# Windowed attention layers on one core: the norm's floor as a maximum over pairs, its first guess on ScalarE, and a new order of four VectorE pieces

## The chip, the cores and the metric

The kernel runs on one core of a Trainium2 chip. The metric is the device time of one execution in microseconds; lower is better. Given are three runs of the kernel before and one profiled execution.

## What is computed

The input x has 4 sequences of 512 tokens with 128 channels. Six parts follow each other on it: a feed-forward part with sign weights, a rotary attention, the same feed-forward part, a stack of six windowed layers, a delta-rule memory, and the same stack of six windowed layers again. The change touches the two stacks alone. One layer of the stack:

```python
def attn_layer(x, Wqkv, qs, ksc, Wo):          # 16 heads of 64, window 32
    q, k, v = split(x @ Wqkv)
    q = l2norm(q) * qs
    k = l2norm(k) * ksc                        # l2norm(t) = t / max(|t|, 1e-12)
    q = q * cos * scale + rotate_half(q) * sin * scale
    k = k * cos * inv + rotate_half(k) * sin * inv
    return local_attention(q, k, v) @ Wo       # softmax(8 * q k^T) v over 64 keys

def ffn_layer(x, g, bln, W1, b1, W2, b2):
    xn = (x - mean(x)) / sqrt(var(x) + 1e-5) * g + bln
    a, gate = split(xn @ W1 + b1)
    return a * gelu(gate) @ W2 + b2

for i in range(6):
    x = attn_layer(shift_tokens(x), ...) + x
    x = ffn_layer(shift_tokens(x), ...) + x
```

## The kernel before

`windowed_layers` runs one stack. It walks over tiles of 128 tokens: a layer has 16 of them (4 sequences of 4 tiles), a stack 96, and there are two stacks, `run` 0 and 1. Each turn of the walk is a step k, and in a step each engine works on several tiles of different ages: T is new, A one step old, B two, C three, D four. `walk` writes steps 0 to 11 out, then two turns of a loop over 32 steps, then the rest. The order of each engine's work in a step is written out by hand in its `step` function; engines meet at semaphores only.

For a tile, TensorE projects the queries of 16 heads (`project`, L251) into PSUM; ScalarE squares them (`square`, L477) into `squares`; VectorE rotates them (`rotate`: L574 with the cosines, L579 with the sines) into `turned`, which frees PSUM for the keys; then the same for the keys. VectorE sums the squares of a head (`sum_squares`, L583) into `sumsq`, 16 numbers for the queries, 16 for the keys; four more columns hold the variances of a feed-forward layer norm (L643). So 36 inverse square roots are wanted per step. VectorE raises `sumsq` to at least 1e-24 (L654, the floor), makes the first guess by integer arithmetic on the bits (L656) and -0.5 times the sum (`halved`, L657). GpSimd does three Newton steps of four instructions (`invert_roots`, L713 to L723), in the next step of the walk. GpSimd also adds the two parts of the rotation (`add`, L703) and multiplies by the inverse norms (`normalise`, L732).

Attention for older tiles: TensorE transposes queries and keys of B (`turn`, L257), ScalarE copies them out (L511, L518); `scores` (L269, L277) gives the scores of B, VectorE takes the negated maximum (L661) and adds it (L667) into `probs`. One step later, for what is then C, ScalarE takes exp (L506), VectorE the row sums (L602) and their inverse (L606), GpSimd multiplies (L740, `pool_p`), VectorE transposes (`pT`, L623), TensorE multiplies by the tokens (`gather`, L287), ScalarE copies to `px` (L481) and TensorE applies the merged weights (`output`, L295).

The feed-forward part of a sequence is spread over steps by k mod 4. At k mod 4 = 3 VectorE adds the attention's result to Z (L679) and TensorE does the up products of an earlier sequence (L415, with `hidden`, L595, on VectorE between them). At 0 TensorE does the down product (L317), VectorE adds it to Z (L616), and TensorE centres the next sequence (L356) and takes its variance (L374). At 1 it broadcasts the inverse deviation (L403), after which VectorE forms `xn` (L588). At 2 come the gate products (L410).

TensorE's order in a step: project the queries of T; transpose the queries of B; `place_0` (the down product, or tokens transposed, L264, which at k mod 4 = 2 wait for `xn`); five pairs of `output`; transpose the keys of B; more `output`; `place_1` (centring, first gate or up product); project the keys of T, which waits for the first rotation; `gather`; `place_2`; the last `output`; `scores`; `place_3`.

VectorE's order in a step: row sums and inverse of C; rotation of the queries of T; at 0 the additions into Z; transposition of C; square sums of the queries; hidden rows; rotation of the keys; square sums of the keys; floor, guess and halves; maximum and difference of B; `xn`, the last hidden rows, or the additions of the attention's result.

Of the kernel before, what the change touches and what calls it, by code (L numbers as in the profile page):

```python
# [6 lines left out]
P = 128  # L7
# [3 lines left out]
I32 = mybir.dt.int32  # L11
ALU = mybir.AluOpType
ACT = mybir.ActivationFunctionType
AXX = mybir.AxisListType.X
# [3 lines left out]
TILES = SEQ // P  # L18
PER = BATCH * TILES
EPS = 1e-5  # L20

DEPTH, HEADS, DH, WIN = 6, 16, 64, 32
# [7 lines left out]
FFB = -(-FF // P)  # L30
VEC = 3 + 2 * FFB
MASKED = -3.0e38
ROOT_BITS, NEWTONS = 0x5F3759DF, 3


EDGE = 96
# [102 lines left out]
def windowed_layers(nc, run, sem, Z, consts, dram):  # L139
# [6 lines left out]
    with ctx:  # L146
        def sb(name, shape, dt=F32):
            return ctx.enter_context(nc.sbuf_tensor(f"{tag}_{name}", shape, dt))
# [14 lines left out]
        rot_l = sb("rot_l", [P, 2, 2, 2, TILES, DH])  # L163
        squares = sb("squares", [P, 2, INNER])
        turned = sb("turned", [P, 2, 2, INNER])
        sumsq = sb("sumsq", [P, NORMS])
        bits = sb("bits", [P, NORMS], I32)
        newton = sb("newton", [P, NORMS])
        halved = sb("halved", [P, NORMS])
        c_1_5, c_zero, c_seed = sb("c_1_5", [P, NORMS]), sb("c_zero", [P, NORMS]), sb("c_seed", [P, NORMS])  # L170
        inv_norm = sb("inv_norm", [P, NORMS])
        rstd = sb("rstd", [P, TILES])
        qk = sb("qk", [P, 2, 2, INNER])
# [6 lines left out]
        row_inv = sb("row_inv", [P, HEADS])  # L180
        pT = sb("pT", [P, 2, HEADS, WIN])
        px = sb("px", [P, 2, WINS, HEADS, WIN])
        warm = sb("warm", [P, 1])
        xn = sb("xn", [P, SEQ])
        xn_sq = sb("xn_sq", [P, SEQ])
        hid = sb("hid", [P, FFB, SEQ])
# [6 lines left out]
        pe_cen, pe_var, pe_bc, pe_gate = sem("pe_cen"), sem("pe_var"), sem("pe_bc"), sem("pe_gate")  # L193
        pe_up, pe_down, pe_bias = sem("pe_up"), sem("pe_down"), sem("pe_bias")
        act_sq, act_tq, act_tk, act_xt = sem("act_sq"), sem("act_tq"), sem("act_tk"), sem("act_xt")
        act_px, act_exp, act_m = sem("act_px"), sem("act_exp"), sem("act_m")
        act_cen, act_gate, act_gelu = sem("act_cen"), sem("act_gate"), sem("act_gelu")
        dve_turn, dve_ss, dve_floor, dve_guess = [sem(s) for s in ("dve_turn", "dve_ss", "dve_floor", "dve_guess")]
        dve_max, dve_sub, dve_sum, dve_inv, dve_pt = sem("dve_max"), sem("dve_sub"), sem("dve_sum"), sem("dve_inv"), sem("dve_pt")
        dve_y, dve_var, dve_xn, dve_hid, dve_z, dve_bias = [  # L200
            sem(s) for s in ("dve_y", "dve_var", "dve_xn", "dve_hid", "dve_z", "dve_bias")]
# [270 lines left out]
        def _(act):  # L472
# [27 lines left out]
            def step(s):  # L500
                T, B, C, D = s.T, s.B, s.C, s.D
                if T:
                    square(T, 0, pe_q)
                if C:
                    act.wait_ge(dve_sub, C.n + 1)
                    nc.scalar.activation(probs[:], probs[:], ACT.Exp).then_inc(act_exp, 1)  # L506
                if B:
                    act.wait_ge(pe_tq, B.n + 1)
                    if C:
                        act.wait_ge(pe_s, C.n + 1)  # L510
                    nc.scalar.activation(flat(qT[:]), flat(ps_t[:]), ACT.Copy).then_inc(act_tq, 1)  # L511
                    if s.k % TILES:
                        tokens_out(B)
                    act.wait_ge(pe_tk, B.n + 1)
                    if s.k == B_LAG:
                        act.wait_ge(cleared, run + 1)
                    turned_k = ps_t[:, :, :].rearrange("p a (b q) -> p (a b) q", q=P)
                    nc.scalar.activation(kT[:, :, HALO + B.t * P:HALO + (B.t + 1) * P], turned_k,  # L518
                                         ACT.Copy).then_inc(act_tk, 1)
                if s.up:  # L520
                    f = s.up
                    act.wait_ge(act_gate, f.m * FFB + FFB)
                    nc.scalar.activation(flat(hid[:]), flat(hid[:]), ACT.Gelu).then_inc(act_gelu, 1)
                if s.merge():
                    layer, parity, quarters = s.merge()
                    merged(layer, parity, quarters[0])
                if s.cen:
                    f = s.cen
                    act.wait_ge(pe_cen, f.m + 1)
                    nc.scalar.activation(xn_sq[:], ps_f[:], ACT.Square)  # L530
                    nc.scalar.activation(xn[:], ps_f[:], ACT.Copy).then_inc(act_cen, 1)
                if s.gate:
                    gate(s.gate, 0)
                if T:
                    square(T, 1, pe_k)
                if C:
                    act.wait_ge(pe_px, C.n + 1)
                    if D and D.k:
                        act.wait_ge(pe_y, D.n)
                    gathered(C, 0)  # L540
                if s.merge():
                    merged(layer, parity, quarters[1])
                if s.gate:
                    gate(s.gate, 1)
                if C:
                    gathered(C, 1)
                if s.up:
                    nc.scalar.activation(warm[:], c_1_5[:, 0:1], ACT.Exp)
                if s.gate:
                    gate(s.gate, 2)  # L550
                if B and s.k % TILES == 0:
                    tokens_out(B)

            walk(act, run, step)

        @block.vector
        def _(dve):
# [3 lines left out]
            ends = Z[:, EDGE:EDGE + BATCH * SPAN].rearrange("p (b t) -> p b t", b=BATCH)  # L561
            nc.vector.memset(ends[lower, :, SEQ:SPAN], 0.0)
            nc.vector.memset(ends[upper, :, 0:1], 0.0)
            nc.vector.memset(c_zero[:], 0.0)
            nc.vector.memset(c_seed[:], float(ROOT_BITS))
            nc.vector.memset(sumsq[:], 1.0).then_inc(edged, 1)
            dve.wait_ge(edged, run + 1)

            def rotate(T, which):
# [10 lines left out]
                                        swapped, sin, ALU.mult).then_inc(dve_turn, 1)  # L580

            def sum_squares(T, which):
                nc.vector.reduce_sum(sumsq[:, which * HEADS:(which + 1) * HEADS], squares[:, which, :]  # L583
                                     .rearrange("p (h d) -> p h d", d=DH), AXX).then_inc(dve_ss, 1)

            def normal(f):
# [10 lines left out]

            def step(s):
                T, A, B, C, D = s.T, s.A, s.B, s.C, s.D
                if C:  # L600
                    dve.wait_ge(act_exp, C.n + 1)
                    nc.vector.reduce_sum(row_sum[:], probs[:], AXX).then_inc(dve_sum, 1)  # L602
                    dve.wait_ge(dve_sum, C.n + 1)
                    if D:
                        dve.wait_ge(pool_p, C.n)
                    nc.vector.reciprocal(row_inv[:], row_sum[:]).then_inc(dve_inv, 1)  # L606
                if T:
                    if T.k % PER == 0:
                        dve.wait_ge(pool_rot, T.layer + 1)
                    rotate(T, 0)  # L610
                if s.down:
                    f = s.down
                    dve.wait_ge(pe_down, f.m + 1)
# [5 lines left out]
                if C:  # L619
                    dve.wait_ge(pool_p, C.n + 1)  # L620
                    if D:
                        dve.wait_ge(pe_px, D.n + 1)
                    nc.vector.transpose(pT[:].rearrange("p a h q -> p h a q"),  # L623
                                        probs[:].rearrange("p h (a k) -> p h a k", a=2)).then_inc(dve_pt, 1)
                if T:
                    if s.chain_before is not None:
                        dve.wait_ge(dve_guess, s.chain_before + 1)
                    sum_squares(T, 0)
                if s.up:
                    hidden(s.up, 0)  # L630
                if s.bias():
# [8 lines left out]
                if s.cen:  # L640
                    f = s.cen
                    dve.wait_ge(pe_var, f.m + 1)
                    nc.vector.tensor_scalar(sumsq[:, 2 * HEADS:NORMS], ps_f[:, 0:TILES], EPS, None,  # L643
                                            ALU.add).then_inc(dve_var, 1)
                if T:
                    sum_squares(T, 1)
                if s.chain is not None:
                    if T:
                        dve.wait_ge(dve_ss, T.n * 2 + 2)
                    if s.cen:  # L650
                        dve.wait_ge(dve_var, s.cen.m + 1)
                    if s.k:
                        dve.wait_ge(pool_inv, s.chain)
                    nc.vector.scalar_tensor_tensor(sumsq[:], sumsq[:], 1e-24, sumsq[:], ALU.max, ALU.max).then_inc(dve_floor, 1)  # L654
                    dve.wait_ge(dve_floor, s.chain + 1)
                    nc.vector.scalar_tensor_tensor(bits[:], sumsq[:].bitcast(I32), -0.5, c_seed[:], ALU.mult, ALU.add)  # L656
                    nc.vector.scalar_tensor_tensor(halved[:], sumsq[:], -0.5, c_zero[:], ALU.mult,  # L657
                                                   ALU.add).then_inc(dve_guess, 1)
                if B:
                    dve.wait_ge(pe_s, B.n + 1)  # L660
                    nc.vector.tensor_reduce(neg_max[:], ps_heads, AXX, ALU.max, negate=True).then_inc(dve_max, 1)  # L661
# [24 lines left out]
        def _(pool):  # L686
# [17 lines left out]
                                        ALU.add).then_inc(pool_add, 1)  # L704

            def invert_roots(chain, bc):
                pool.wait_ge(dve_guess, chain + 1)
                y = bits[:].bitcast(F32)
                for k in range(NEWTONS):
                    at = chain * (4 * NEWTONS - 1) + 4 * k  # L710
# [1 line left out]
                        pool.wait_ge(pool_newton, at)  # L712
                    nc.gpsimd.tensor_tensor(newton[:], y, y, ALU.mult).then_inc(pool_newton, 1)  # L713
                    pool.wait_ge(pool_newton, at + 1)
                    nc.gpsimd.tensor_tensor(newton[:], newton[:], halved[:], ALU.mult).then_inc(pool_newton, 1)
                    pool.wait_ge(pool_newton, at + 2)
                    nc.gpsimd.tensor_tensor(newton[:], newton[:], c_1_5[:], ALU.add).then_inc(pool_newton, 1)
                    pool.wait_ge(pool_newton, at + 3)
                    if bc and k == NEWTONS - 1:
                        rows = slice(2 * HEADS, NORMS)  # L720
# [39 lines left out]
def rotary_tables():  # L760
# [8 lines left out]
    both = lambda a, b: np.concatenate([a, b], -1)  # L769
    cos, sin = np.cos(freqs), np.sin(freqs)  # L770
    rows = []
    for s in (8.0 * scale, 1.0 / scale):
        rows.append([both(cos * s, cos * s), both(-sin * s, sin * s)])
    rows = np.array(rows).astype(np.float32)
    rows = rows.reshape(2, 2, TILES, P, DH).transpose(3, 0, 1, 2, 4)
# [1424 lines left out]
```

## Time and profile before

| | |
|---|---|
| three runs | 4502.45 us median (4500.79 to 4517.26) |
| profiled execution | 4515.56 us, of which the span is 4513.4 us |
| TensorE busy | 4068.2 us (90%) |
| VectorE busy | 3318.9 us (74%) |
| GpSimd busy | 2748.9 us (61%) |
| ScalarE busy | 2057.4 us (46%) |
| mean granted TensorE clock | 0.936 of full |

The two stacks take about 1650 us each (from 560 to 2215 us and from 2775 to 4415 us of the span); there the granted clock is 0.99. Shares of busy time are means over the whole span, the stacks' waits are in the rows below. PEld is TensorE's weight load. Times are microseconds from the span's start unless said otherwise.

### The profile page before, as it was taken

How to read it: one execution, taken by the hardware profiler on the slowest of the kernel's cores; microseconds unless marked ns; L12 is line 12 of the kernel's file. 1: busy time of each engine (PE TensorE's matmuls, PEld its weight loads, DVE VectorE, ACT ScalarE, POOL GpSimd, SP SyncE). 2: the span in 40 equal slices, each digit the busy share in tenths (PEclk: the TensorE clock that was granted, in tenths of full speed). 3: DMA queues.
4: the chain of work that ended last, by engine and by line, in shares of the span. 5: the costliest groups of instructions: out<-in, count | busy, mean ns of one | idle time of the engine just before them, and what ended most of it. 6: DMA issues, size and time to landing. Idle time of an engine off the chain costs nothing. (4 is left out here: it accounts for less than half of the span.)

```text
span 4513.4 us, 129963 instructions
## 1 busy us (share of the span) xinstructions
PE 4068.2 (90%) x56144; PEld 2601.6 (58%) x56144; DVE 3318.9 (74%) x3855; ACT 2057.4 (46%) x2429; POOL 2748.9 (61%) x3481
## 2 busy tenths in 40 slices
PE   8999889999999999999867776999999999999996
PEld 4333456566666666666536663666656666666663
DVE  1575288888888888888734334888888888888883
ACT  2454245554545555555421112455555555554552
POOL 0000188777777777777614124878777777787781
PEclk9999899999999999999976556999999999999997
DMA  0000100000000000000000001000000000000000
GB/s 18 1 1 1 47 11 11 11 16 11 2 17 11 16 11 2 7 2 2 2 7 4 4 4 57 11 11 2 17 11 17 12 2 17 11 7 2 2 2 10
DMA packets 14118, 46.29 MB, mean 10 GB/s; under 512 B 3808, under 2 KB 6240, under 8 KB 11744
## 3 DMA queue, kind: packets, MB, share of 16 engines
q1 hardware_dynamic: 13536, 37.83, 2.4%
q8 instruction: 450, 7.37, 0.7%
q14 instruction: 132, 1.08, 0.1%
HBM read 36.78 MB, written 1.05 MB: 8 GB/s over the span
## 5 line engine op out<-in xcount | busy, mean ns | idle before, releaser
L703 POOL TENSOR_TENSOR w_qk<-w_turned 128x1024 f32<-128x1024 f32 x384 | 906.7, 2361 | 152.9 <-DVE w_turned L579 151.7
L251 PE MATMUL w_ps_qk<-w_w_qk,ZT 128*128 128x512 f32 x1536 | 764.0, 621 | 74.5 <-DVE w_turned L579 52.0
L295 PE MATMUL w_ps_y<-w_px,w_w_vo 128*128 128x128 f32 x6144 | 788.3, 277 | 6.1 <-DVE ZT L679 6.1
L295 PEld LDWEIGHTS w_ps_y<-w_px,w_w_vo 128*128 128x128 f32 x6144 | 744.1, 192 | 80.4 <-issue 76.6
L477 ACT ACTIVATE w_squares<-w_ps_qk 128x1024 f32<-128x1024 f32 x384 | 393.4, 1024 | 753.0 <-PE w_ps_qk L251 753.0
L732 POOL TENSOR_TENSOR w_qk<-w_qk,w_inv_norm 128x1024 f32<-128x1024 f32 x384 | 723.0, 1905 | 0.0
L574 DVE TENSOR_TENSOR w_turned<-w_ps_qk,w_rot_l 128x1024 f32<-128x1024 f32 x384 | 467.4, 1217 | 239.5 <-ACT w_squares L477 213.7
L740 POOL TENSOR_TENSOR w_probs<-w_probs,w_row_inv 128x1024 f32<-128x1024 f32 x192 | 365.5, 1904 | 347.1 <-DVE w_row_inv L606 346.5
L251 PEld LDWEIGHTS w_ps_qk<-w_w_qk,ZT 128*128 128x128 f32 x1536 | 281.9, 195 | 404.0 <-issue 312.0
L481 ACT ACTIVATE w_px<-w_ps_w 128x1024 f32<-128x1024 f32 x384 | 379.2, 1021 | 199.8 <-PE w_ps_w L287 199.8
L579 DVE TENSOR_TENSOR w_turned<-w_ps_qk,w_rot_l 128x1024 f32<-128x1024 f32 x384 | 466.1, 1214 | 0.0
L583 DVE TENSOR_REDUCE w_sumsq<-w_squares 128x16 f32<-128x1024 f32 x384 | 458.2, 1193 | 0.0
L257 PEld LDWEIGHTS w_ps_w<-ident,w_qk 128*128 128x128 f32 x3072 | 353.5, 142 | 128.8 <-issue 128.7
L257 PE MATMUL w_ps_w<-ident,w_qk 128*128 128x128 f32 x3072 | 403.1, 275 | 22.7 <-ACT w_qT L511 22.5
L287 PE MATMUL w_ps_w<-w_pT,w_x_tok 32*128 32x512 f32 x3072 | 389.7, 622 | 13.4 <-issue 8.3
L518 ACT ACTIVATE w_kT<-w_ps_w 128x1024 f32<-128x1024 f32 x192 | 196.7, 1024 | 386.8 <-PE w_ps_w L257 386.8
L602 DVE TENSOR_REDUCE w_row_sum<-w_probs 128x16 f32<-128x1024 f32 x192 | 234.3, 1220 | 188.2 <-ACT w_probs L506 187.1
L690 POOL TENSOR_TENSOR w_rot_l<-w_rot,w_qk_scale 128x256 f32<-128x256 f32 x24 | 17.5, 729 | 533.3 <-DMA w_qk_scale<-in_qk_scale 533.3
L277 PEld LDWEIGHTS w_ps_w<-w_kT,w_qT 64*32 64x32 f32 x24576 | 256.3, 105 | 126.7 <-issue 126.7
L277 PE MATMUL w_ps_w<-w_kT,w_qT 64*32 64x64 f32 x24576 | 292.2, 225 | 40.4 <-issue 40.4
L654 DVE SCALAR_TENSOR_TENSOR w_sumsq<-w_sumsq 128x36 f32<-128x36 f32 x196 | 283.4, 1446 | 6.8
L287 PEld LDWEIGHTS w_ps_w<-w_pT,w_x_tok 32*128 32x128 f32 x3072 | 140.8, 186 | 247.2 <-issue 245.6
(247 smaller groups left out, 6314.8 us busy)
## 6 DMA issues: line engine op xcount, KB each, us to landing
w_w_qk<-in_w_qk SPq DMA_DIRECT2D x12, 1024.0 KB, 4.8
w_w_vT<-in_w_vT SPq DMA_DIRECT2D x12, 512.0 KB, 4.1
w_w_o<-in_w_o SPq DMA_DIRECT2D x12, 512.0 KB, 5.1
w_w<-in_w SPq DMA_DIRECT2D x12, 384.0 KB, 3.2
w_w<-in_w SPq DMA_DIRECT2D x12, 192.0 KB, 3.2
XT<-in_x SPq DMA_DIRECT2D x1, 1024.0 KB, 4.8
w_rot<-in_rot SPq DMA_DIRECT2D x2, 512.0 KB, 5.7
out<-XT SPq DMA_DIRECT2D x1, 1024.0 KB, 3.9
```

The lines of the kernel that those rows point to most:

```text
L251: last = nc.tensor.matmul(ps_qk[:, c, :], Z[:, T.col:T.col + P], w_qk[:, T.parity, cols], start=True, stop=True)
L257: last = nc.tensor.transpose(ps_t[:, p // 4, (p % 4) * P:(p % 4 + 1) * P], qk[:, B.odd, which, p * P:(p + 1) * P], ident[:])
L277: last = nc.tensor.matmul(ps_heads[w * WIN:(w + 1) * WIN, h * PAIRS + p, :], qT[rows, p, w * WIN:(w + 1) * WIN], kT[rows, p, col:col + KEY ...
L287: last = nc.tensor.matmul(ps_w[:, w, :], x_tok[rows, C.t, half, :], pT[rows, half].rearrange("p h q -> p (h q)"), start=half == 0, stop=ha ...
L295: last = nc.tensor.matmul(ps_y[:, D.t * P:(D.t + 1) * P].rearrange("p (w q) -> p w q", q=WIN), w_vo[:, D.parity, h, p, :], px[:, D.odd, :, ...
L477: nc.scalar.activation(squares[:, which, :], flat(ps_qk[:]), ACT.Square).then_inc(act_sq, 1)
L481: nc.scalar.activation(px[:, C.odd, pair].rearrange("p w h q -> p (w h q)"), flat(ps_w[:, pair, :]), ACT.Copy).then_inc(act_px, 1)
L574: nc.vector.tensor_tensor(turned[:, which, 0, :].rearrange("p (h d) -> p h d", d=DH), flat(ps_qk[:]).rearrange("p (h d) -> p h d", d=DH), ...
L579: nc.vector.tensor_tensor(turned[:, which, 1, :].rearrange("p (h two d) -> p h two d", two=2, d=HALF), swapped, sin, ALU.mult).then_inc(dv ...
L583: nc.vector.reduce_sum(sumsq[:, which * HEADS:(which + 1) * HEADS], squares[:, which, :] .rearrange("p (h d) -> p h d", d=DH), AXX).then_i ...
L703: nc.gpsimd.tensor_tensor(qk[:, T.odd, which, :], turned[:, which, 0, :], turned[:, which, 1, :], ALU.add).then_inc(pool_add, 1)
L732: nc.gpsimd.tensor_tensor(heads, heads, spread(inv, 2, [P, HEADS, DH]), ALU.mult).then_inc(pool_qk, 1)
```

## The change

The floor and the guess: `sumsq` gets a second column beside each number, filled once with 1e-24, and the floor becomes one reduction by maximum over the pairs into a tensor `floor`. The guess moves from VectorE to ScalarE: one activation (identity, scale -0.5, a bias) on the bits of `floor`, behind ScalarE's second copy to `px`, waiting for the floor; GpSimd waits for it there. `halved` goes: the square roots are taken of half the value (the variances are halved at their making, the constant of the guess is shifted by half an exponent, the query table carries 16 in place of 8), and GpSimd's third Newton instruction becomes a subtraction from 1.5.

The order on VectorE: the rotation of the queries now stands ahead of the row sums of C, and the square sums of the queries right behind the inverse, ahead of the additions into Z and the transposition.

```diff
-ROOT_BITS, NEWTONS = 0x5F3759DF, 3
+ROOT_BITS, NEWTONS = 0x5F3759DF - 0x400000, 3
...
-        sumsq = sb("sumsq", [P, NORMS])
+        sumsq, floor, seed = sb("sumsq", [P, NORMS, 2]), sb("floor", [P, NORMS]), sb("seed", [P, 1])
...
                 if s.up:
-                    nc.scalar.activation(warm[:], c_1_5[:, 0:1], ACT.Exp)
+                    nc.scalar.activation(warm[:], warm_in[:], ACT.Exp)
+                if s.chain is not None:
+                    act.wait_ge(dve_floor, s.chain + 1)
+                    if s.k:
+                        act.wait_ge(pool_inv, s.chain)
+                    nc.scalar.activation(bits[:], floor[:].bitcast(I32), ACT.Identity, bias=seed[:, 0:1],
+                                         scale=-0.5).then_inc(act_guess, 1)
                 if s.gate:
                     gate(s.gate, 2)
...
                 T, A, B, C, D = s.T, s.A, s.B, s.C, s.D
+                if T:
+                    if T.k % PER == 0:
+                        dve.wait_ge(pool_rot, T.layer + 1)
+                    rotate(T, 0)
                 if C:
                     dve.wait_ge(act_exp, C.n + 1)
                     nc.vector.reduce_sum(row_sum[:], probs[:], AXX).then_inc(dve_sum, 1)
...
                     nc.vector.reciprocal(row_inv[:], row_sum[:]).then_inc(dve_inv, 1)
                 if T:
-                    if T.k % PER == 0:
-                        dve.wait_ge(pool_rot, T.layer + 1)
-                    rotate(T, 0)
+                    if s.chain_before is not None:
+                        dve.wait_ge(dve_floor, s.chain_before + 1)
+                    sum_squares(T, 0)
                 if s.down:
...
-                if T:
-                    if s.chain_before is not None:
-                        dve.wait_ge(dve_guess, s.chain_before + 1)
-                    sum_squares(T, 0)
                 if s.up:
                     hidden(s.up, 0)
...
-                    nc.vector.scalar_tensor_tensor(sumsq[:], sumsq[:], 1e-24, sumsq[:], ALU.max, ALU.max).then_inc(dve_floor, 1)
-                    dve.wait_ge(dve_floor, s.chain + 1)
-                    nc.vector.scalar_tensor_tensor(bits[:], sumsq[:].bitcast(I32), -0.5, c_seed[:], ALU.mult, ALU.add)
-                    nc.vector.scalar_tensor_tensor(halved[:], sumsq[:], -0.5, c_zero[:], ALU.mult,
-                                                   ALU.add).then_inc(dve_guess, 1)
+                    nc.vector.tensor_reduce(floor[:], sumsq[:], AXX, ALU.max).then_inc(dve_floor, 1)
...
-                pool.wait_ge(dve_guess, chain + 1)
+                pool.wait_ge(act_guess, chain + 1)
...
-                    nc.gpsimd.tensor_tensor(newton[:], newton[:], halved[:], ALU.mult).then_inc(pool_newton, 1)
+                    nc.gpsimd.tensor_tensor(newton[:], newton[:], floor[:], ALU.mult).then_inc(pool_newton, 1)
...
-                    nc.gpsimd.tensor_tensor(newton[:], newton[:], c_1_5[:], ALU.add).then_inc(pool_newton, 1)
+                    nc.gpsimd.tensor_tensor(newton[:], c_1_5[:], newton[:], ALU.subtract).then_inc(pool_newton, 1)
```

## Rows read from the trace of the kernel before

**Rows 1.** Waits of the whole span: engine, line, releaser: total us, times, longest us
```profile
PE w_ps_qk L251 <- DVE w_turned L579: 52.0, 50, 2.4
...
PE w_ps_f L317 <- DVE w_hid L595: 44.7, 38, 2.8
...
PE w_ps_w L277 <- issue: 40.4, 31, 2.1
...
PE w_ps_f L264 <- DVE w_xn L588: 36.6, 38, 1.7
```

**Rows 2.** Timeline of TensorE, four steps of run 1: start, us, line, [idle before]
```profile
3528.58 1.88 PE L251 MATMUL w_ps_qk<-w_w_qk,ZT 128*128 128x512 f32 x4
...
3536.46 1.98 PE L251 MATMUL w_ps_qk<-w_w_qk,ZT 128*128 128x512 f32 x4
3538.37 2.00 PE L287 MATMUL w_ps_w<-w_pT,w_x_tok 32*128 32x512 f32 x16
...
3544.13 1.99 PE L251 MATMUL w_ps_qk<-w_w_qk,ZT 128*128 128x512 f32 x4
...
3548.45 0.44 PE L264 MATMUL w_ps_f<-ident,ZT 128*128 128x128 f32 x2 [1.46 <-DVE w_xn L588]
...
3555.39 2.00 PE L287 MATMUL w_ps_w<-w_pT,w_x_tok 32*128 32x512 f32 x16
...
3561.63 1.88 PE L251 MATMUL w_ps_qk<-w_w_qk,ZT 128*128 128x512 f32 x4
...
3571.40 2.00 PE L287 MATMUL w_ps_w<-w_pT,w_x_tok 32*128 32x512 f32 x16
...
3577.63 1.88 PE L251 MATMUL w_ps_qk<-w_w_qk,ZT 128*128 128x512 f32 x4
...
3581.48 2.84 PE L317 MATMUL w_ps_f<-w_hid,w_w 128*128 128x512 f32 x6 [1.09 <-DVE w_hid L595]
...
3588.12 1.13 PE L356 MATMUL w_ps_f<-ZT,centre 128*128 128x512 f32 x2 [0.25 <-DVE ZT L616]
...
3590.89 2.00 PE L287 MATMUL w_ps_w<-w_pT,w_x_tok 32*128 32x512 f32 x16
...
3596.93 1.88 PE L251 MATMUL w_ps_qk<-w_w_qk,ZT 128*128 128x512 f32 x4
```

**Rows 3.** Timeline of VectorE in the same stretch
```profile
3543.05 1.88 DVE L654 SCALAR_TENSOR_TENSOR w_sumsq<-w_sumsq 128x36 f32<-128x36 f32 x1
...
3545.19 1.22 DVE L661 TENSOR_REDUCE w_neg_max<-w_ps_w 128x16 f32<-128x1024 f32 x1
3546.51 1.23 DVE L667 TENSOR_TENSOR w_probs<-w_ps_w,w_neg_max 128x1024 f32<-128x1024 f32 x1
...
3548.86 1.22 DVE L602 TENSOR_REDUCE w_row_sum<-w_probs 128x16 f32<-128x1024 f32 x1 [0.47 <-ACT w_probs L506]
...
3551.45 1.22 DVE L579 TENSOR_TENSOR w_turned<-w_ps_qk,w_rot_l 128x1024 f32<-128x1024 f32 x1
3552.58 1.24 DVE L623 STREAM_TRANSPOSE w_pT<-w_probs 128x1024 f32<-128x1024 f32 x1
3553.74 1.18 DVE L583 TENSOR_REDUCE w_sumsq<-w_squares 128x16 f32<-128x1024 f32 x1
...
3581.34 1.38 DVE L679 TENSOR_TENSOR ZT<-w_ps_y,ZT 64x512 f32<-64x512 f32 x2
...
3586.56 1.50 DVE L616 SCALAR_TENSOR_TENSOR ZT<-w_ps_f,w_vec,ZT 64x512 f32<-64x512 f32 x2
```

**Rows 4.** Timeline of ScalarE in the same stretch
```profile
3546.23 1.02 ACT L477 ACTIVATE w_squares<-w_ps_qk 128x1024 f32<-128x1024 f32 x1 [3.77 <-PE w_ps_qk L251]
```

**Rows 5.** Timeline of GpSimd in the same stretch
```profile
3542.51 2.37 POOL L703 TENSOR_TENSOR w_qk<-w_turned 128x1024 f32<-128x1024 f32 x1
...
3550.51 1.91 POOL L740 TENSOR_TENSOR w_probs<-w_probs,w_row_inv 128x1024 f32<-128x1024 f32 x1 [1.22 <-DVE w_row_inv L606]
```

**Rows 6.** The page's group of the folded scales: busy, mean ns, idle before
```profile
L690 POOL TENSOR_TENSOR w_rot_l<-w_rot,w_qk_scale 128x256 f32<-128x256 f32 x24 | 17.5, 729 | 533.3 <-DMA w_qk_scale<-in_qk_scale 533.3
```

More of the change, by code:

```diff
@@ L165, in windowed_layers @@
         turned = sb("turned", [P, 2, 2, INNER])
-        sumsq = sb("sumsq", [P, NORMS])
+        sumsq, floor, seed = sb("sumsq", [P, NORMS, 2]), sb("floor", [P, NORMS]), sb("seed", [P, 1])
         bits = sb("bits", [P, NORMS], I32)
         newton = sb("newton", [P, NORMS])
-        halved = sb("halved", [P, NORMS])
-        c_1_5, c_zero, c_seed = sb("c_1_5", [P, NORMS]), sb("c_zero", [P, NORMS]), sb("c_seed", [P, NORMS])
+        c_1_5 = sb("c_1_5", [P, NORMS])
         inv_norm = sb("inv_norm", [P, NORMS])
@@ L195, in windowed_layers @@
         act_sq, act_tq, act_tk, act_xt = sem("act_sq"), sem("act_tq"), sem("act_tk"), sem("act_xt")
-        act_px, act_exp, act_m = sem("act_px"), sem("act_exp"), sem("act_m")
+        act_px, act_exp, act_m, act_guess = sem("act_px"), sem("act_exp"), sem("act_m"), sem("act_guess")
         act_cen, act_gate, act_gelu = sem("act_cen"), sem("act_gate"), sem("act_gelu")
-        dve_turn, dve_ss, dve_floor, dve_guess = [sem(s) for s in ("dve_turn", "dve_ss", "dve_floor", "dve_guess")]
+        dve_turn, dve_ss, dve_floor = sem("dve_turn"), sem("dve_ss"), sem("dve_floor")
         dve_max, dve_sub, dve_sum, dve_inv, dve_pt = sem("dve_max"), sem("dve_sub"), sem("dve_sum"), sem("dve_inv"), sem("dve_pt")
@@ L552, in step @@
                     tokens_out(B)
+            act.wait_ge(edged, run + 1)
             walk(act, run, step)
@@ L563, in _ @@
             nc.vector.memset(ends[upper, :, 0:1], 0.0)
-            nc.vector.memset(c_zero[:], 0.0)
-            nc.vector.memset(c_seed[:], float(ROOT_BITS))
-            nc.vector.memset(sumsq[:], 1.0).then_inc(edged, 1)
+            nc.vector.memset(warm_in[:], 0.0)
+            nc.vector.memset(sumsq[:, :, 0], 1.0)
+            nc.vector.memset(sumsq[:, :, 1], 1e-24)
+            nc.vector.memset(seed[:], float(ROOT_BITS)).then_inc(edged, 1)
             dve.wait_ge(edged, run + 1)
@@ L582, in sum_squares @@
             def sum_squares(T, which):
-                nc.vector.reduce_sum(sumsq[:, which * HEADS:(which + 1) * HEADS], squares[:, which, :]
+                nc.vector.reduce_sum(sumsq[:, which * HEADS:(which + 1) * HEADS, 0], squares[:, which, :]
                                      .rearrange("p (h d) -> p h d", d=DH), AXX).then_inc(dve_ss, 1)
@@ L642, in step @@
                     dve.wait_ge(pe_var, f.m + 1)
-                    nc.vector.tensor_scalar(sumsq[:, 2 * HEADS:NORMS], ps_f[:, 0:TILES], EPS, None,
-                                            ALU.add).then_inc(dve_var, 1)
+                    nc.vector.tensor_scalar(sumsq[:, 2 * HEADS:NORMS, 0], ps_f[:, 0:TILES], EPS, 0.5,
+                                            ALU.add, ALU.mult).then_inc(dve_var, 1)
                 if T:
@@ L771, in rotary_tables @@
     rows = []
-    for s in (8.0 * scale, 1.0 / scale):
+    for s in (16.0 * scale, 1.0 / scale):
         rows.append([both(cos * s, cos * s), both(-sin * s, sin * s)])
```

2 lines of the change are left out of this document (1 added, 1 removed).

## The prediction

> **What bounds the kernel now.** The page and the waits first: in them TensorE's longest waits on another engine inside the windowed layers are three, on VectorE each time: 52.0 us for the rotation (L579) ahead of the projection, 44.7 us for the hidden rows ahead of the down product, 36.6 us for `xn` ahead of the transposes of the tokens. A fourth, 40.4 us, stands ahead of the scores and is put down to no one ("issue") [rows 1]. Then TensorE's timeline over four steps. I number the kinds of step by k mod 4: 1 broadcasts, 2 gates, 3 multiplies up, 0 multiplies down and centres. P is the start of a step's first projection (L251), G that of its gather (L287). Kind 1: P 3528.58, G at P+9.79, next P at P+15.55. Kind 2: G at P+11.26, next P at +17.50. Kind 3: +9.77 and +16.00. Kind 0: +13.26 and +19.30 [rows 2]. From G to the next P TensorE runs its own list without a wait: 5.76, 6.24, 6.23 and 6.04 us. So a step costs G-P plus that constant, and the question is what sets G. Before G, kind 1 waits for the rotation (second projection at P+7.88), kind 2 for `xn` (1.46 us), kind 0 for `hid` (1.09 us) and for Z (0.25 us), kind 3 for nothing to speak of [rows 2]. TensorE sets the pace with VectorE a hair behind it: VectorE is not full, but it is late at three places.
>
> Why it is late at two of them is in VectorE's rows. The floor (L654, 36 columns) took 1.88 us and ended at 3544.93, when GpSimd's addition (L703, from 3542.51, 2.37 us) ended at 3544.88. The reduction of 1024 columns (L583) took 1.18 us while the same GpSimd line ran beside it [rows 3, 5]. The maximum over the scores (L661) started at 3545.19, though the scores were done about 3544.2, when the next projection began.
>
> The Trainium skill, page "SBUF — State Buffer", section "Who interferes with whom", says that a VectorE instruction with two SBUF inputs is held while a GpSimd instruction reads SBUF, and that tensor_reduce never contends on trn2. The first half is what these rows show. By the second the new floor is free of it; if the reduction were held too, the time would be that of the third rival below.
>
> **The change part by part.**
> *Floor and guess.* Three VectorE instructions go (L654, here 1.88 us, and L656 and L657, which fit into the 0.26 us between L654's end and L661's start), and one reduction of 72 columns comes. L583 takes 1.18 us for 1024 columns; scaled, that is 0.08, and the whole of it is the other end; I take 0.2, an estimate near the small end, since two small instructions fit into those 0.26 us [rows 3]. VectorE gets about 1.9 us here, but L661 can only start when the scores are done: in kind 2 that is 1.0 us earlier than now. The guess goes to ScalarE, behind its second copy to `px`. It waits there for the floor; behind it queue the last gate copy, `tokens_out` and the next step's square. The square starts at 3546.23, the floor would be done by 3543.3 [rows 3, 4], so a guess of 0.2 to 1.0 us (the square of 1024 columns takes 1.02) holds up nobody. GpSimd can start its Newton steps as soon as L703 ends instead of 0.47 us later: no cost. GpSimd's subtraction, the doubled constants and the tables in `rot` have the same shapes: nothing.
>
> The Trainium skill, page "ScalarE: Activation LUTs", section "Table sets: the hidden batching unit", says that the cheap functions, identity among them, lie in every table set; by that the guess brings no table load. No row quoted here shows more of it; with a load the guess would be later and the sum the same as long as it ends before the next square.
>
> *Rotation ahead of the row sums.* This is the part that costs. Now: square of the first projection starts at P+2.10 (3546.23), exp of the scores behind it (L667's end at 3547.74 to the row sum at 3548.86: 1.12 us), so the row sum starts about P+4.0 where ScalarE's order sets it (P+4.73 in kind 2, where L667 was late), then 1.65 us to GpSimd's multiplication (3548.86 to 3550.51), which takes 1.91, then 0.16, then the transposition 1.24. So pT is there 4.96 us after the row sum starts: at P+8.96, where TensorE's own order reaches the gather at P+9.77 [rows 2 to 5]. That was 0.8 us of cover. New: the square ends at P+3.12 by this row, or P+3.02 when the projection is 1.88 long; the rotation is two pieces of 1.22 us, and neighbours overlap by 0.08 (L579 ends at 3552.67, L623 starts at 3552.58): 2.36 us, P+3.05 to P+5.41; the row sum starts at P+5.33 [rows 3]; pT is there at P+10.29, the gather starts at P+10.33. The rotation has become part of the chain projection, square, rotation, row sum, inverse, GpSimd's multiplication, transposition, gather. The cover is gone and 0.55 us is owed.
>
> *Sum of squares behind the inverse.* 1.18 us, in the shadow of GpSimd's 1.91 us in kinds 1, 2 and 3, where VectorE waited for that product anyway under the new order: nothing. In kind 0 it stands ahead of the two additions into Z (1.50 us), for which TensorE's centring waits.
>
> *Per step.*
> Kind 1: the wait for the rotation ends at P+5.5, well ahead of need; the gather is bound by pT at P+10.33 instead of 9.79: +0.54.
> Kind 3: 10.33 for 9.77: +0.56.
> Kind 2: L661 starts right after the scores at P+0.1, L667 at +1.4 and ends at +2.65, `xn` is done at +3.3 (0.75 us, as long as one half of L616); TensorE's wait for it falls from 1.46 to about 0.6; the rotation starts at +3.3, pT is there at +10.5. G at P+10.5 instead of 11.26: -0.76. But this is the best case of kind 2. The 36.6 us over 48 such steps are 0.76 us on the mean, not 1.46 [rows 1]; where the wait was small the gather is bound by pT as in the other kinds. I take -0.76 + 0.70 = -0.06 for the mean step.
> Kind 0: the scores end about P-0.9, since one product of 512 columns lies between (half a projection, 0.94); L661 starts at about -0.7, L667 ends at +1.85, the last hidden rows (0.75, estimated as for `xn`) at +2.5: TensorE's wait for `hid` (1.09) is gone. Then the y additions (1.38) to P+3.8, rotation to +6.15, row sum to +7.3, inverse to +7.6, sum of squares to +8.7, Z to +10.2. The centring (L356) stood at P+10.49 (3588.12 less 3577.63) and now stands at +10.22. Of 1.09 us saved ahead of it all but 0.27 are given back: -0.27 [rows 2, 3].
>
> There are 48 steps of each kind (2 runs, 6 layers, 16 steps a layer): 48 x (0.54 - 0.06 + 0.56 - 0.27) = 48 x 0.77 = +37 us. At k mod 16 = 6 GpSimd also folds the scales (L690, 0.73 us twice, and four half-sized pieces of 0.36 to 0.73: 2.9 to 4.4 us [rows 6]). It delays its Newton steps and with them the multiplication now on the chain; ten times 0.5 us, +5. Sum +42 us. Against it: the 40.4 us ahead of the scores that nobody releases [rows 1] fall between gather and scores; a TensorE that now stands up to 1.9 us before the gather may have its instructions at hand by then. That is worth 0 to -40 us; the opposite, that these pauses were hidden in part by the `xn` and `hid` waits that go, 0 to +14. I take -14, a third of the first end. Net +28 us. The profiled execution took 4515.56 us, 4513.4 of it span and 2.2 around it, which the change leaves alone; it lies 0.3% over the median of the runs shown. 28 of 4515.56 is 0.62%; on the median 4502.45 that is 4530 us. This case's own range is 4504 (all 40 us gained) to 4558 (none gained, +14 paid).
>
> **The rivals.**
> *Faster: the gather is covered after all.* If pT came by P+9.77, for instance because the row sum slips in ahead of the rotation or the chain's handoffs are shorter than I add them, only the savings count: the three waits of 52.0, 44.7 and 36.6 us, 133 us at most, about 100 with the Z wait left: some 4400 us. It decides at 0.55 us, the amount by which my chain overshoots TensorE's own order. Against it: VectorE's order is fixed in the program, and each link of the chain is a row. 0.13, with half savings (4450) inside it.
> *No difference: pauses absorbed.* The full 40 us ahead of the scores go, or kind 0 gains its whole 1.09: 4490 to 4515 us. 0.20.
> *The floor does not get free.* If the reduction over pairs is held by GpSimd as L654 was, kinds 2 and 0 keep their lateness and pay the later row sum too: about 1.0 us more in each, 96 us at worst, 60 with cover: 4585 us. Against it: L583, one SBUF input, is never stretched beside L703 [rows 3, 5]. 0.07.
> *GpSimd becomes the bound.* Its own list is Newton, 4.0 us (L703's end 3544.88 to L740's start 3550.51, less 0.47 and 1.22 of idle time; the 0.47 is the wait for L657), then 1.91 + 2.37 + 3.8 (two of L740's size) + 2.37 [rows 5]: 14.5 us of steps of 16 to 19; a late multiplication pushes the next. It decides when a step has under 14.5 us, or where the fold (17.5 with it) meets kind 3. If it cost 0.3 us in every step: 4590 us. 0.04.
> The forecast's case keeps 0.56.
>
> **How the numbers follow.** Likeliest 4530 us. The range 4468 to 4575 leaves out the fast rival's bulk and the far ends of the slow ones, 2 in 10. A measurement of this kernel can tell about 0.5% from no change, 22.5 us: 4480 to 4525. Faster: the first rival, 0.13. Within: the second, and of the forecast's case the part under 4525, about 0.33 of it: 0.20 + 0.18 = 0.38, less a little for its tail: 0.37. Slower: 0.50.
>
> **What would show it.** The floor's mean near 0.2 us and the maximum over the scores starting within 0.2 us of the scores' end. TensorE's waits for `hid` gone, for the rotation gone, for `xn` more than halved. In their place a wait of TensorE at L287 for pT (L623): about 1.9 us in plain kind 1, 0.6 in kind 3, 0.1 to 0.6 in kind 2, none in kind 0, some 30 to 45 us in all per run; a longer wait for Z at L356. Steps of 16.1, 16.7, 16.6 and 19.0 us. I am wrong if L287 waits for nothing, if kind 0 falls under 18.5 us, or if the floor's duration still follows L703.

## The result: slower by 1.1%

The changed kernel takes 4557.01 us (median of 4 runs, 4551.45 to 4564.55) against 4503.48 us for the kernel before (4 runs): ratio 1.0114, 95% interval 1.0087 to 1.0141. The forecast was 4530 us, slower; the range went to 4575. So the sign and the mechanism held, and the size was about half of what came: 53.5 us between the medians where 28 were forecast. Between the two profiled executions it is 4552.70 less 4515.56, 37 us: the profiled run before lay 12 us over its median.

The page of the changed kernel, engines and two groups:

```profile
PE 4046.1 (89%) x56144; PEld 2615.8 (57%) x56144; DVE 3026.4 (67%) x3465; ACT 2099.3 (46%) x2625; POOL 2731.5 (60%) x3481
...
L286 PE MATMUL w_ps_w<-w_pT,w_x_tok 32*128 32x512 f32 x3072 | 400.9, 636 | 155.4 <-DVE w_pT L634 146.8
...
L634 DVE STREAM_TRANSPOSE w_pT<-w_probs 128x1024 f32<-128x1024 f32 x192 | 239.1, 1245 | 157.5 <-POOL w_probs L743 156.1
```

VectorE lost 292 us of work (3318.9 to 3026.4) and the kernel got slower. The last number of these two groups says where: the gather (L286) stood idle 146.8 us for `pT`, and the transposition that makes `pT` (L634) stood idle 156.1 us for GpSimd's multiplication. In the kernel before these two waits were 5.1 and 11.6 us. TensorE's waits, the list that answers to [rows 1]:

```profile
PE w_ps_w L286 <- DVE w_pT L634: 146.8, 144, 2.5
PE w_ps_f L355 <- DVE ZT L627: 49.8, 44, 1.6
PE w_ps_w L276 <- issue: 42.0, 34, 2.8
PE w_ps_qk L250 <- DVE w_turned L586: 16.4, 10, 1.9
```

The rotation's 52.0 us became 16.4. The wait for the hidden rows fell from 44.7 to 6.1 us, the one for `xn` from 36.6 to 13.6. The wait for Z ahead of the centring (L355) rose from 16.8 to 49.8, as the prediction said it would rise. The 40.4 us ahead of the scores are 42.0. And 146.8 us stand at the gather in 144 of 192 steps: three kinds of step out of four. TensorE's timeline over the same steps of kinds 2, 3 and 0 as in [rows 2]:

```profile
3563.88 1.98 PE L250 MATMUL w_ps_qk<-w_w_qk,ZT 128*128 128x512 f32 x4
...
3567.31 0.44 PE L263 MATMUL w_ps_f<-ident,ZT 128*128 128x128 f32 x2 [0.58 <-DVE w_xn L595]
...
3574.52 2.00 PE L286 MATMUL w_ps_w<-w_pT,w_x_tok 32*128 32x512 f32 x16 [0.19 <-issue]
...
3580.75 1.88 PE L250 MATMUL w_ps_qk<-w_w_qk,ZT 128*128 128x512 f32 x4
...
3591.26 2.00 PE L286 MATMUL w_ps_w<-w_pT,w_x_tok 32*128 32x512 f32 x16 [0.94 <-DVE w_pT L634]
...
3597.49 1.88 PE L250 MATMUL w_ps_qk<-w_w_qk,ZT 128*128 128x512 f32 x4
...
3607.50 1.12 PE L355 MATMUL w_ps_f<-ZT,centre 128*128 128x512 f32 x2 [1.12 <-DVE ZT L627]
...
3610.27 2.00 PE L286 MATMUL w_ps_w<-w_pT,w_x_tok 32*128 32x512 f32 x16
...
3616.30 1.88 PE L250 MATMUL w_ps_qk<-w_w_qk,ZT 128*128 128x512 f32 x4
```

The letters are those of the prediction: P is the start of a step's first projection, G that of its gather, and the kind of a step is k mod 4. Kind 2: G at P+10.64, step 16.87. Kind 3: P+10.51, step 16.74. Kind 0: the centring at P+10.01, G at P+12.78, step 18.81. From G to the next P there are 6.23, 6.23 and 6.03 us, as before. VectorE in the step of kind 3 (P = 3580.75):

```profile
3583.90 1.23 DVE L581 TENSOR_TENSOR w_turned<-w_ps_qk,w_rot_l 128x1024 f32<-128x1024 f32 x1 [1.45 <-ACT w_squares L476]
3585.04 1.22 DVE L586 TENSOR_TENSOR w_turned<-w_ps_qk,w_rot_l 128x1024 f32<-128x1024 f32 x1
3586.17 1.21 DVE L613 TENSOR_REDUCE w_row_sum<-w_probs 128x16 f32<-128x1024 f32 x1
3587.41 0.26 DVE L617 RECIPROCAL w_row_inv<-w_row_sum 128x16 f32<-128x16 f32 x1
3587.58 1.16 DVE L590 TENSOR_REDUCE w_sumsq<-w_squares 128x16 f32<-128x1024 f32 x1
3589.75 1.25 DVE L634 STREAM_TRANSPOSE w_pT<-w_probs 128x1024 f32<-128x1024 f32 x1 [1.01 <-POOL w_probs L743]
```

Here is the whole chain: VectorE is idle 1.45 us for the square, rotates, takes the row sum only at P+5.42, and later waits 1.01 us for GpSimd. `pT` is there at 3591.00, P+10.25, and the gather starts 0.26 us after that.

The means of all steps from the fifth on (44 or 46 of a kind), in us, from the starts of the first projection and of the gather in either trace; change and forecast are those of the step:

| kind (k mod 4) | G-P before, after | step before, after | change | forecast |
|---|---|---|---|---|
| 1 | 9.78, 10.46 | 16.38, 17.33 | +0.95 | +0.54 |
| 2 | 10.61, 10.54 | 17.16, 17.15 | -0.01 | -0.06 |
| 3 | 9.98, 10.55 | 16.67, 17.20 | +0.53 | +0.56 |
| 0 | 13.03, 12.60 | 19.16, 18.79 | -0.37 | -0.27 |

### The profile page after: what moved, and what is told of

It is laid out like the page before. It is cut to its first block and busy times, and to the rows that moved or that the text cites. A ratio compares the mean times of both kernels' runs of the same rounds, so it can differ in the third digit from the quotient of the medians.

```text
span 4550.9 us, 129901 instructions
## 1 busy us (share of the span) xinstructions
PE 4046.1 (89%) x56144; PEld 2615.8 (57%) x56144; DVE 3026.4 (67%) x3465; ACT 2099.3 (46%) x2625; POOL 2731.5 (60%) x3481
## 5 line engine op out<-in xcount | busy, mean ns | idle before, releaser
L250 PE MATMUL w_ps_qk<-w_w_qk,ZT 128*128 128x512 f32 x1536 | 750.7, 612 | 37.8 <-DVE w_turned L586 16.4
L743 POOL TENSOR_TENSOR w_probs<-w_probs,w_row_inv 128x1024 f32<-128x1024 f32 x192 | 365.1, 1902 | 591.2 <-DVE w_row_inv L617 590.7
L286 PE MATMUL w_ps_w<-w_pT,w_x_tok 32*128 32x512 f32 x3072 | 400.9, 636 | 155.4 <-DVE w_pT L634 146.8
L664 DVE TENSOR_REDUCE w_neg_max<-w_ps_w 128x16 f32<-128x1024 f32 x192 | 235.1, 1225 | 291.9 <-PE w_ps_w L276 286.6
L286 PEld LDWEIGHTS w_ps_w<-w_pT,w_x_tok 32*128 32x128 f32 x3072 | 156.2, 189 | 387.6 <-issue 385.9
L634 DVE STREAM_TRANSPOSE w_pT<-w_probs 128x1024 f32<-128x1024 f32 x192 | 239.1, 1245 | 157.5 <-POOL w_probs L743 156.1
```

The costliest lines, as they stand in the source:

```text
L250: last = nc.tensor.matmul(ps_qk[:, c, :], Z[:, T.col:T.col + P], w_qk[:, T.parity, cols], start=True, stop=True)
L286: last = nc.tensor.matmul(ps_w[:, w, :], x_tok[rows, C.t, half, :], pT[rows, half].rearrange("p h q -> p (h q)"), start=half == 0, stop=ha ...
```

## The experiments

The theory: the new floor and guess gain, the new order loses more, and it loses at the gather through the chain projection, square, rotation, row sum, inverse, multiplication, transposition. Seven kernels take it apart. Ratios are to the kernel before, run again beside them: 4512.71 us (13 runs) for the first four, 4510.16 us (7 runs) for the last three.

**The floor and guess alone.** The changed kernel with VectorE's old order (this cut and those below are shortened; T, C and `s.down` stand for the tiles and sequences of the step):

```diff
 def step(s):
-    if T: rotate(T, 0)
     if C: row sums, inverse
+    if T: rotate(T, 0)
-    if T: sum_squares(T, 0)
     if s.down: additions into Z
     if C: transposition
+    if T: sum_squares(T, 0)
```

> The new floor and guess with VectorE's old order (row sums first, square sums behind the transposition). My theory (the order costs, the floor gains): steps of kind 1 stay at 15.55 us, kind 2 loses most of its 0.76 us wait for xn, kind 3 is unchanged, kind 0 loses its 1.09 us wait for the hidden rows and the centring starts about 1.3 us earlier; the gather waits for pT in almost no step. In all about -75 us: ratio to before 0.983 (0.977 to 0.990). Rival (the wait at the gather comes from the guess on ScalarE or from the new floor, not from the order): near the changed kernel, 1.008 to 1.012.

Measured: 4429.38 us, ratio 0.9818 (0.9801 to 0.9834). TensorE's waits there:

```profile
PE w_ps_qk L250 <- DVE w_turned L586: 53.5, 50, 2.4
PE w_ps_w L276 <- issue: 34.4, 26, 1.9
PE w_ps_f L355 <- DVE ZT L623: 20.2, 43, 1.6
...
PE w_ps_w L286 <- DVE w_pT L630: 14.4, 10, 2.6
...
PE w_ps_f L263 <- DVE w_xn L595: 13.5, 26, 0.5
```

The ratio is where the theory put it. The gather's wait falls from 146.8 to 14.4 us by the order of VectorE alone; the guess on ScalarE is in this kernel and makes nothing late. Kind 0 takes 18.15 us on the mean (19.16 before), kind 2 16.63 (17.16), kinds 1 and 3 are unchanged (16.34 and 16.60). So the floor and guess were worth 1.8%, and the order cost 1.0114 over 0.9818, 3.0%.

**The order alone.** The kernel before, floor, guess and halves untouched, with the new order of the four pieces (the reverse of the diff above, in the kernel before).

> The new order alone, with the kernel before's floor, guess and halves. My theory: the floor still ends when GpSimd's addition ends, which the late multiplication has itself pushed back; the maximum over the scores starts 1.4 to 2.0 us after the scores in kinds 1 and 2. In all 60 to 115 us over the changed kernel: ratio to before 1.025 to 1.037. Rival (the floor is in the shadow once the order is new, VectorE has time to spare): as the changed kernel, 1.011.

Measured: 4647.59 us, ratio 1.0295 (1.0278 to 1.0312). The two halves make up the whole: 0.9818 x 1.0295 = 1.0108, and the whole change measured 1.0114. The size was forecast right and the place wrong. The excess over the changed kernel was expected in kinds 1 and 2; it is mostly in kind 0, 20.09 us on the mean against 18.79. Kind 2 has 17.52 against 17.15, kind 3 17.33 against 17.20, kind 1 nothing. The maximum starts late behind the scores of kinds 2 and 3 (1.58 and 1.42 us on the mean, 0.65 and 0.43 behind the others), so it is the steps after these that find VectorE late. What holds the floor is seen in a step where GpSimd has two pieces queued (VectorE, then GpSimd):

```profile
3637.23 0.84 DVE L654 SCALAR_TENSOR_TENSOR w_sumsq<-w_sumsq 128x36 f32<-128x36 f32 x1
3638.10 2.28 DVE L656 SCALAR_TENSOR_TENSOR w_bits<-w_sumsq,w_c_seed 128x36 int32<-128x36 int32 x1
```

```profile
3634.26 3.76 POOL L732 TENSOR_TENSOR w_qk<-w_qk,w_inv_norm 128x1024 f32<-128x1024 f32 x2
3637.98 2.36 POOL L703 TENSOR_TENSOR w_qk<-w_turned 128x1024 f32<-128x1024 f32 x1
```

The floor ends at 3638.07, when the normalisation ends (3638.02); the guess ends at 3640.38, when the addition ends (3640.34). With two GpSimd instructions behind each other, two small VectorE instructions are held in a row.

**The squares back.** The changed kernel, the square sums of the queries behind the transposition again, the rotation still first.

> The changed kernel with the square sums of the queries back behind the transposition; the rotation stays first. My theory: kinds 1, 2 and 3 as in the changed kernel (gather at P+10.5), in kind 0 the additions into Z start 1.2 us earlier and the wait of 1.1 us for them ahead of the centring shrinks to 0.5 or less; part is lost again since the hidden rows come later. In all -29 us against the changed kernel: ratio to before 1.003 to 1.007. Rival (the square sums hide behind GpSimd's multiplication in the new place and are exposed in the old): 1.013 or more.

Measured: 4526.83 us, ratio 1.0027 (1.0015 to 1.0039). The gather's wait stays at 147.0 us in 143 steps, and the wait for Z ahead of the centring is gone from the first entries. Kind 0 takes 18.04 us on the mean (18.79), the others stay within 0.08 us. So of the order's 3.0% the square sums ahead of Z are 0.9% and the rotation ahead of the row sums is 2.1%. The forecast band began at 1.003: the move gained a hair more than expected.

**The reduction alone.** The kernel before with its floor as the reduction over pairs; guess and halves stay on VectorE.

```diff
-nc.vector.scalar_tensor_tensor(sumsq[:], sumsq[:], 1e-24, sumsq[:], ALU.max, ALU.max)
+nc.vector.tensor_reduce(floor[:], sumsq[:], AXX, ALU.max)
-nc.vector.scalar_tensor_tensor(bits[:], sumsq[:].bitcast(I32), -0.5, c_seed[:], ALU.mult, ALU.add)
+nc.vector.scalar_tensor_tensor(bits[:], floor[:].bitcast(I32), -0.5, c_seed[:], ALU.mult, ALU.add)
...
```

> The kernel before with only its floor exchanged for the reduction over pairs; guess and halves stay on VectorE and read two SBUF operands each. Port theory: the floor takes 0.2 us, and the guess behind it (L656's successor) is now the one that ends when GpSimd's addition ends, mean about 1.4 us; time as before, ratio 0.998 to 1.002. Rival (it was the floor's own arithmetic or write that was slow): guess stays at 0.2 us and the time falls as with guess on ScalarE, 0.983.

Measured: 4493.26 us, ratio 0.9957 (0.994 to 0.9974). VectorE's groups in it:

```profile
L657 DVE SCALAR_TENSOR_TENSOR w_bits<-w_floor,w_c_seed 128x36 int32<-128x36 int32 x196 | 235.8, 1203 | 7.1 <-DVE w_floor L655 0.4
L655 DVE TENSOR_REDUCE w_floor<-w_sumsq 128x36 f32<-128x72 f32 x196 | 44.7, 228 | 6.8
```

The wait moved to the next instruction with two operands in SBUF: the guess, 0.22 us on the mean in the kernel before, takes 1.20 here, and the reduction 0.23. The time is a little better than the "as before" of the expectation, by 0.4%: floor and guess together take 1.43 us on the mean instead of 1.67, and TensorE's waits for the hidden rows and for `xn` fell to 35.3 and 27.5 us. It is the pair, floor as a reduction and guess off VectorE, that is worth 1.8%; the reduction alone brings a quarter of it.

The Trainium skill, page "SBUF — State Buffer", section "Who interferes with whom", has this rule: two SBUF inputs contend with a reading GpSimd, tensor_reduce does not. These rows agree on both halves.

**The product out of the chain.** The changed kernel, but GpSimd's multiplication writes a tensor that nobody reads, and VectorE transposes the unscaled exponentials behind the inverse. The output lacks the division by the row sums.

```diff
-nc.gpsimd.tensor_tensor(probs[:], probs[:], spread(row_inv[:], 2, [P, HEADS, KEYS]), ALU.mult)
+nc.gpsimd.tensor_tensor(scaled[:], probs[:], spread(row_inv[:], 2, [P, HEADS, KEYS]), ALU.mult)
...
 if C:                                    # the transposition
-    dve.wait_ge(pool_p, C.n + 1)
...
 if C:                                    # ahead of the next tile's difference into probs
     dve.wait_ge(dve_pt, C.n + 1)
+    dve.wait_ge(pool_p, C.n + 1)
```

> The changed kernel with GpSimd's multiplication by the inverse row sums taken out of the chain: it writes a tensor that nobody reads, and VectorE transposes the unscaled exponentials right behind the inverse, so the output lacks the division by the row sums. All instructions stay. Theory (TensorE's new wait is the chain projection, square, rotation, row sum, inverse, multiplication, transposition): the 146.8 us at the gather go nearly all, G-P falls to about 8.5 in plain kind 1, 9.7 in kinds 2 and 3 and stays in kind 0, where Z sets it: ratio to before 0.976 (0.970 to 0.983). Rival (the gather waits for something else that the change made late): 1.008 to 1.012.

Measured: 4422.07 us, ratio 0.9804 (0.9786 to 0.9822).

```profile
PE w_ps_f L356 <- DVE ZT L628: 52.2, 44, 1.6
PE w_ps_w L277 <- issue: 40.3, 30, 2.1
PE w_ps_w L287 <- DVE w_pT L634: 23.2, 22, 1.2
```

The gather waits 23.2 us instead of 146.8, and the ratio falls from 1.0114 to 0.9804, 3.1% of the time, with every instruction still there. In kind 3 G is at P+9.49 (median), TensorE's own order. In kind 1 it stays at +9.43 on the mean. In three of four of these steps TensorE's own list reaches the gather at +9.46 to +9.53 without a wait for `pT`. In the fourth (k mod 16 = 1), for which I had +8.5, it still waits. Here is one (P = 3528.45), VectorE, then TensorE:

```profile
3535.28 1.16 DVE L591 TENSOR_REDUCE w_sumsq<-w_squares 128x16 f32<-128x1024 f32 x1
3536.36 1.23 DVE L634 STREAM_TRANSPOSE w_pT<-w_probs 128x1024 f32<-128x1024 f32 x1
```

```profile
3537.84 2.00 PE L287 MATMUL w_ps_w<-w_pT,w_x_tok 32*128 32x512 f32 x16 [1.14 <-DVE w_pT L634]
```

With the multiplication out of the way VectorE's own list sets `pT`: the square sums stand ahead of the transposition, which ends at P+9.14. Kind 0 keeps its wait for Z. This is the direct test: what holds the gather in the changed kernel is the chain with the multiplication in it.

**Two steps further.** First the additions into Z ahead of the rotation, on top of the floor with the old order:

```diff
     if C: row sums, inverse
+    if s.down: additions into Z
     if T: rotate(T, 0)
-    if s.down: additions into Z
```

> The kernel with the new floor and VectorE's old order, and at k mod 4 = 0 the additions into Z ahead of the rotation of the queries, behind the inverse. Theory: the centring waits for Z by 0.48 us there because the rotation stands ahead of it; Z can start when the down product ends, about P+5.5, so the wait goes and the second projection, 0.4 us earlier, still finds the rotation done. -0.47 us in each of 48 steps, -22 us: ratio to before 0.977 (0.974 to 0.980). Rival: the rotation, now 1.5 us later, delays the transposition and the gather; 0.982 or more.

Measured: 4409.48 us, ratio 0.9777 (0.9755 to 0.98). Kind 0 takes 17.50 us on the mean (18.15), and the wait for Z is gone from the first entries. The ratio is in the expected band; its interval and that of the kernel without this move (0.9801 to 0.9834) just don't touch. Then TensorE's order as well:

```diff
+    if not s.gate:
         place_0(s)
     if D: output(D, range(5))
+    if s.gate:
+        place_0(s)
...
-    last_pairs = 7 if s.gate or s.up else 6
+    last_pairs = 7 if s.gate or s.up else 8 if s.bc and not s.merge() and not s.bias() else 6
...
```

> The same, and on TensorE at k mod 4 = 2 the transposes of the tokens behind the first five pairs of the output in place of ahead of them, and at k mod 4 = 1 (where no weights are merged and no bias is made) the last two pairs of the output ahead of the second projection. Theory: the wait for xn (0.5 us in half of the steps of kind 2) and the wait for the rotation (1.3 us in the plain steps of kind 1) are filled with work that has to be done anyway: -13 and -16 us, ratio to before 0.970 (0.966 to 0.975). Rival: the waits move on to the gather or the scores, 0.977.

Measured: 4398.27 us, ratio 0.9758 (0.9742 to 0.9774); the gain is smaller than the band that was given, and the rival's 0.977 lies in the interval too. TensorE's waits with Z ahead of the rotation:

```profile
PE w_ps_qk L250 <- DVE w_turned L586: 53.2, 50, 2.4
PE w_ps_w L276 <- issue: 35.3, 28, 2.0
...
PE w_ps_f L263 <- DVE w_xn L595: 13.5, 26, 0.5
```

and with TensorE's order too:

```profile
PE w_ps_w L276 <- issue: 40.8, 29, 1.9
PE w_ps_qk L250 <- DVE w_turned L591: 39.5, 50, 2.4
```

The gather did not take the waits over (13.2 us, 14.3 without the move). The wait of the token transposes for `xn` (13.5 us) is gone from the first entries and the wait for the rotation fell by 13.7, 27 us together; 11 us came out between the medians, and the two intervals overlap. The pauses ahead of the scores stand at 40.8 us against 35.3; the rest of the difference isn't placed. This is the fastest kernel of the study, 2.4% under the kernel before.

## Why the prediction was right, and where its sizes were off

**The chain.** The step that carried the forecast held: the rotation became part of the chain to the gather. Predicted G at P+10.33 in kinds 1 and 3, measured 10.46 and 10.55 on the mean. `pT` was forecast for P+10.29 and came at P+10.25 in the step shown. The cover of 0.8 us was read rightly too: in the kernel before `pT` is there at P+8.96 (median of kinds 1 and 3) and the gather starts at +9.77. What I mis-sized is the link behind it: 0.04 us from `pT` to the gather, where the trace shows 0.26 (3591.00 to 3591.26). The kernel before showed it in two steps only, since its gather had no wait to end. 0.2 us in 144 steps are 29 us. The trace also shows what lies in it. The gather waits for four semaphores, the centring for one. After `pT` TensorE's queue runs two more semaphore instructions, L454 at 3591.04 and L455 at 3591.15, before the first weight load of the gather at 3591.23, though the semaphores other than that of `pT` had been set by 3587.92. Ahead of the centring there is none, and it starts 0.05 us after Z. No run tried another order of these waits.

**Kind 1.** +0.95 us for +0.54. 0.68 is G (0.14 more than forecast, the link above); 0.27 lies behind it, which the sum took for a constant. Less than 0.1 of that are the pauses ahead of the scores. About 0.2 is TensorE's clock: in kind 1 the gather took 0.16 us longer on the mean, and the broadcast behind it a little. One such step, TensorE's timeline, then the window of its gather (us, PE busy, PEclk, DMA share, GB/s):

```profile
4187.23 1.88 PE L250 MATMUL w_ps_qk<-w_w_qk,ZT 128*128 128x512 f32 x4
4191.20 3.69 PE L286 MATMUL w_ps_w<-w_pT,w_x_tok 32*128 32x512 f32 x16 [2.09 <-DVE w_pT L634]
```

```profile
4191.20:4194.60 3.40, 3.40 (x16) 0.51 0.02 5
```

TensorE stood idle for 2.09 us, the granted clock then fell from 2.4 to 1.2 GHz, and the gather took 3.69 us where it takes 2.00. This came in 6 of the 46 steps of kind 1, each after an idle time of 2.08 to 2.24 us, and in none of the kernel before; 10 others waited 2.08 to 2.33 us and kept the clock. So a wait on the busiest engine cost more than its own length. The prediction had no term for it.

**Kind 3.** +0.53 for +0.56, on the mean. A step without a pause went from 16.00 to 16.74, +0.74; the difference is steps of the kernel before that were late already.

**Kind 2.** The wait for `xn` fell from 1.46 to 0.58 us in the step that was laid out; forecast 0.6. G at +10.64 for +10.5. The mean moved by -0.01 for -0.06.

**Kind 0.** The wait for `hid` went and came back as a wait for Z: L355 waits 1.12 us, the centring is at P+10.01 where +10.22 was forecast. -0.37 for -0.27 on the mean. The experiment with the squares put back gives 0.75 us of it back, so the price of that move, hidden in the other kinds, was rightly put in kind 0 alone.

**The pauses ahead of the scores.** Here the sum was wrong. I took -14 us for them, because a waiting TensorE might use the time. They measured 42.0 us after 40.4: nothing was absorbed. Without that term the forecast would have been +42. The traces show more of these pauses than their length. Count everything that TensorE's queue ran (weight loads, matmuls, its own instructions): all 31 pauses of the kernel before and all 34 of the changed one stand at counts that leave one of three remainders (22 or 23, 106 or 107, 194 or 195) when divided by 256, and 24 of the 34 at the very counts of before. So they belong to places in the instruction stream and not to what TensorE waits for, and standing earlier in the step doesn't take them away. That instructions come late there in blocks of 256 is the likely reading; no run tested it.

**The sum.** With the right link 29 us more would be owed, but not all of it shows in the means: in the kernel before many steps of kinds 2 and 3 were late already (a median kind 2 at G = P+10.34, a mean kind 3 at P+9.98), and those had less to lose. 48 times the measured changes of the four kinds, 1.10 us together, is +53 us. That this is also the difference of the medians is chance: between these two traces the stacks differ by 45 us from their first to their last P (the first four steps of a stack got 6 us shorter together) and the spans by 37.5.

**The folded scales.** The +5 us were small and are not confirmed. In the ten steps with the fold G moved by +0.53 us (other steps of kind 2: -0.24), in the ten behind them by +0.17 (other steps of kind 3: +0.68): 0.26 us more per fold, under 3 us, if nothing else sets these steps apart.

**The base.** The sum was scaled by 4502.45 over 4515.56. That moves it by 0.1 us; but the profiled run before was 12 us slow, and a change of 50 us is read off by such a difference as 37 or 53.

**A slip.** The forecast of the gather's wait, "some 30 to 45 us in all", does not follow from its own working: 48 steps of kind 3 at 0.6 us and 48 of kind 2 at 0.1 to 0.6 are 34 to 58 us alone, and kind 1 was to wait up to 1.9. It measured 146.8; from the fifth step on the means were 1.35 us in kind 1, 1.04 in kind 3 and 0.56 in kind 2.

**The rivals.** The fast one (the gather covered after all) fell with the gather's wait in 144 steps. The floor got free: 0.23 us in every step, and the maximum over the scores starts 0.04 to 0.16 us behind the scores on the mean of each kind, where it was 0.45 to 1.23. GpSimd did not become the bound: its multiplication waited 590.7 us for the inverse in the changed kernel, where it had waited 346.5. The guess on ScalarE took 0.32 us and had no table load ahead of it; GpSimd waited for it four times, all at the end of a stack.

## What to carry to other kernels

Before putting a piece of work ahead of another because its input is there earlier, follow what hangs on the one that is pushed back, across all engines, up to the instruction of the busiest engine that ends it, and compare with the time at which that engine would get there anyway. Here 0.8 us of cover hid a chain through three engines; the rotation pushed the row sum back by 1.4 us (from P+4.0 to P+5.42), and 292 us of work taken off VectorE didn't make up for it. Judge such a change by its parts: one half was worth 1.8%, the other cost 3%, and the sum looked like a failed idea.

## What the runs showed of the hardware

- A VectorE instruction (`scalar_tensor_tensor`) on 36 columns with two operands in SBUF takes 0.20 us alone. Where it started beside a running GpSimd instruction it took 1.11 to 2.15 us (the floor, 192 of 196 executions) or 0.84 to 2.30 us (the guess behind the reduction, 192 of 196), and ended 0.05 to 0.06 us after that instruction. The reduction of 72 columns, one operand, took 0.227 to 0.231 us in all 192 executions that started beside one. Exchanging one instruction for the reduction moves the wait to the next that has two operands.
- From the end of VectorE's transposition to the start of the matmuls that read it there are 0.26 us when TensorE stands there waiting, with two semaphore instructions 0.11 us apart in between; for `xn` and Z, with one semaphore on the weight load itself, it was 0.05 us.
- After idle times of 2.08 to 2.24 us TensorE's granted clock fell from 2.4 to 1.2 GHz in 6 of 46 steps of kind 1 (10 with idle times of 2.08 to 2.33 us kept it), and the gather took up to 3.69 us instead of 2.00.
- TensorE's pauses ahead of the scores (40.4 us in 31 places, 42.0 in 34) stand whole multiples of 256 instructions of its queue apart, to within one, inside a stretch of the program.
